# A four-layer graph network on one core: 8-bit rank rows, turns by the transposing form, gathers written out over eight buffers, scatters without a bound

## The chip, the cores and the metric

The kernel runs on one core of one Trainium2 chip. The metric is the device time of one execution in microseconds (us). Engines are named as in the profile: PE (TensorE), DVE (VectorE), ACT (ScalarE), POOL (GpSimd), SP (SyncE); "POOLq", "SPq", "ACTq" are their instruction queues, from which DMAs are issued and in which semaphores are waited for.

## The reference

There are 6250 nodes with 128 features each and 106250 edges, sorted by receiver `dst`; each node has a self-loop. Four layers follow each other, each closed by a residual and a layer norm:

```python
# L0: message = relu([h[src], h[dst], w] @ W1 + b1) @ W2 + b2; agg = segment_max(message, dst); dense update
# L1: message = relu([x[src'], factors[..]] @ Wm + bm); agg = segment_sum; dense update
# L2: attention over 4 heads: alpha = segment softmax of leaky_relu(e_l[src] + e_r[dst]); out = segment_sum(alpha * Wh[src], dst)
# L3: neigh = mean of x[src] by dst; h = relu(x @ W_in[0] + neigh @ W_in[1]); the same again with W_out
x = _layernorm(x + _L0_gnn_ref(x, edge_weight, src, dst, ...))
x = _layernorm(x + _L1_gnn_ref(x, L1_gnn_factors, src, dst, ...))
x = _layernorm(x + _L2_gnn_ref(x, edge_index, ...))
x = _layernorm(x + _L3_gnn_ref(x, L3_gnn_W_in, L3_gnn_W_out, src, dst))
```

All arithmetic is float32.

## The kernel before

Edges are cut into NB = 208 blocks of EB = 512, each of CT = 4 tiles of 128. A sweep walks the 208 blocks; a step is one block. There are five sweeps, each in one program block together with the node phase that follows it (`run(sweep, node_phase(k))`); all engines meet at a barrier between program blocks.

- Sweep k=1 (`edge_phase(1)`, layer L0, "the first sweep"): per block, POOL gathers four times 128 rows of 1 KB from `joint_table` (L1114) into one of SLOTS = 4 buffers `joint`. SP loads the rank and bar rows broadcast over 128 partitions (L1143, one DMA of 256 KB), the receiver rows (L1148, 256 KB) and the edge weights (L1155). DVE makes the 0/1 matrix `same` from rank row and `rank_cols` (L1299). PE adds up, in one bank, weight row (L1191), sender rows times the identity (L1194: turns them) and receiver rows times `same` (L1195); ACT stores the factor half of the buffer back to DRAM (L1238) and applies the relu (L1241); PE multiplies by W2 (L1203), DVE scans with a running max (L1318), PE turns back (L1213), ACT copies (L1255) and stores 256 KB (L1261).
- Relation sweep (`relation_phase`, layer L1): no gather. SP issues five DMAs a step: rank row (L1357, 128 KB broadcast), a 1 KB row (L1358), receiver rows (L1359), factor rows (L1360), and the store of the scan (L1366). PE: a bf16 row product (L1390), factor rows times the identity (L1380), receiver rows times `same` (L1381), and the turn back (L1400).
- Attention sweep (`attention_phase`, L2): gathers of 528-byte rows (L1507) into 16 buffers; stretches of 8 blocks for the softmax.
- Sweeps k=4 and k=5 (`edge_phase(4)`, `edge_phase(5)`, L3): gathers of 512-byte rows (L1114) into 4 buffers, four `transpose` (L1187), a scan, the turn back and the store.

`steps` runs an engine's pieces with lags in a hardware loop; `straight` writes them out. POOL's sweeps run in such loops, with the four index columns of a block copied by ACT into `idx` first (L1226, L1612) and handed over by the semaphores `e_idx` and `t_idx`. In the first sweep POOL waits, before it gathers into a buffer, for `e_gath_free` (L1108) and for the factor store out of that buffer (`factor_out`, L1112).

Node phases: POOL gathers each node's last scan row (L738), as soon as enough blocks are stored (`e_kept`); dense products and layer norm; tables to DRAM; for k = 0, 1, 2 a scatter of the receivers' rows to each segment's first place in `first_d` (L747, with a bounds check, so that the rows of the 22 padding nodes are dropped) and 7 gathers (L761). POOL's scatters and gathers of a node phase are written out.

A matmul of 128 float32 columns times the identity is two PE instructions here; a `transpose` is one (the counts of L1194 and L1187 in the profile: 1664 each, for one and for two sweeps of 832 tiles).

## Time and profile before

| | |
|---|---|
| median of 3 runs | 5793.68 us (5790.52 to 5794.18) |
| the profiled execution | 5795.6 us |
| its span, first to last instruction | 5793.8 us |
| mean granted TensorE clock | 0.735 of full |
| busy share: PE, DVE, ACT, POOL | 59%, 42%, 24%, 63% |
| DMA | 1127.80 MB, mean 195 GB/s |

The stages follow each other in time: preparation and node phase 0 up to 366 us, first sweep 366 to 1470, node phase 1 to 1640, relation sweep to 2228, node phase 2 to 2365, attention to 3432, node phase 3 to 3555, sweep 4 to 4593, node phase 4 to 4670, sweep 5 to 5708, node phase 5 to the end. Averages over the span mix stages with different limits, so the profile is read stage by stage. Of an engine's row, "idle before" is the time that it stood still ahead of such instructions, with what ended it.

### The profile page before, as it was taken

To read this page: it belongs to the slowest core of one execution; us is meant where nothing else is said; L and a number is where in the kernel's file an instruction comes from. 1 tells how busy PE (TensorE), PEld (TensorE's weight loads), DVE (VectorE), ACT (ScalarE), POOL (GpSimd) and SP (SyncE) were. 2 spreads that over 40 slices of the span, in tenths; PEclk is the share of its full clock that TensorE was granted. 3 is DMA by queue.
4 is the path that set the end of the run, shared out by engine and by line. 5 is a ranking of instruction groups with operands and counts; after the bars stand their busy time and mean duration, and the time that the engine had idled before them with its cause. 6 is when DMAs were issued, how large, how long until landed. Compare 5 with 4: busy or idle time off the path is not lost. (4 is left out here: it accounts for less than half of the span.)

```text
span 5793.8 us, 95902 instructions
## 1 busy us (share of the span) xinstructions
PE 3447.0 (59%) x19621; PEld 2711.1 (47%) x19621; DVE 2417.4 (42%) x3906; ACT 1387.4 (24%) x3059; POOL 3658.6 (63%) x3808
## 2 busy tenths in 40 slices
PE   1258988889669998466666662333333443333335
PEld 0246565556458886466656561333333333333333
DVE  3323333333546666366666664222222222222224
ACT  0012222222224443133333231111111211111111
POOL 2267777777611013777777774777777767777776
PEclk9779999999889999588888885555555565555557
DMA  9969999999479997466666653455544444444443
GB/s 231 306 183 291 298 300 301 304 298 296 124 234 332 327 331 231 138 182 181 181 181 186 177 168 87 131 131 131 131 131 131 124 114 131 131 131 131 131 131 106
DMA packets 809797, 1127.80 MB, mean 195 GB/s; under 512 B 128769, under 2 KB 490874, under 8 KB 806362
## 3 DMA queue, kind: packets, MB, share of 16 engines
q1 hardware_dynamic: 368424, 431.55, 24.3%
q0 software_dynamic: 134688, 305.12, 21.5%
q10 hardware_dynamic: 306588, 390.09, 20.2%
q8 instruction: 31, 0.51, 0.0%
q14 instruction: 66, 0.54, 0.0%
HBM read 688.68 MB, written 438.07 MB: 194 GB/s over the span
## 5 line engine op out<-in xcount | busy, mean ns | idle before, releaser
L1114 POOL DMA_INDIRECT gath<-sender_table,idx x1664 | 1570.2, 944 | 577.0 <-issue 413.5
L1318 DVE TENSOR_TENSOR_SCAN scan<-meta,scan,bank 128x512 f32<-128x512 bf16 x624 | 798.6, 1280 | 1943.2 <-DVEq L1315 1942.8
L1187 PE MATMUL bank<-ident,gath 128*128 128x128 f32 x1664 | 464.1, 434 | 1277.5 <-DMA gath<-sender_table,idx 1277.5
L1114 POOL DMA_INDIRECT gath<-joint_table,idx x832 | 810.4, 974 | 298.9 <-issue 208.2
L1507 POOL DMA_INDIRECT gath<-attention_table,idx x832 | 814.1, 978 | 263.3 <-issue 191.7
L1187 PEld LDWEIGHTS bank<-ident,gath 128*128 128x128 f32 x1664 | 297.8, 217 | 1443.5 <-DMA gath<-sender_table,idx 1443.5
L1255 ACT ACTIVATE rows<-bank 128x512 f32<-128x512 f32 x624 | 372.6, 597 | 1149.9 <-ACTq L1253 1121.5
L738 POOL DMA_INDIRECT gath<-scan_rows,end_i x196 | 188.9, 964 | 646.2 <-ACTq L1432 574.7
L1213 PE MATMUL bank<-ident,scan 128*128 128x128 f32 x2496 | 568.6, 373 | 4.5 <-PEq L1211 4.5
L1213 PEld LDWEIGHTS bank<-ident,scan 128*128 128x128 f32 x2496 | 470.6, 202 | 130.5 <-issue 130.5
L1194 PE MATMUL bank<-ident,gath 128*128 128x128 f32 x1664 | 372.5, 309 | 0.0
L1195 PE MATMUL bank<-same,recv 128*128 128x128 f32 x1664 | 353.4, 297 | 0.0
L1194 PEld LDWEIGHTS bank<-ident,gath 128*128 128x128 f32 x1664 | 277.4, 209 | 161.2 <-issue 161.2
L1380 PE MATMUL bank<-ident,gath 128*128 128x128 f32 x1664 | 343.2, 288 | 0.0
L1191 PE MATMUL bank<-small,w1w 1*128 1x512 f32 x416 | 236.5, 648 | 148.4 <-DMA gath<-joint_table,idx 96.5
L1543 PE MATMUL bank<-recv,same 128*128 128x4 f32 x1664 | 225.4, 259 | 156.7 <-PEq L1541 156.4
L1241 ACT ACTIVATE hid<-bank,b 128x512 f32<-128x512 f32 x208 | 143.0, 687 | 698.8 <-ACTq L1240 647.8
L1226 ACT ACTIVATE idx<-src_cols 128x4 int32 (+1 forms) x624 | 127.7, 205 | 754.5 <-ACTq L1265 651.6
L1543 PEld LDWEIGHTS bank<-recv,same 128*128 128x128 f32 x1664 | 217.9, 204 | 184.7 <-issue 184.5
L1771 DVE TENSOR_TENSOR_SCAN scan<-bank,scan,hid 128x512 f32<-128x512 f32 x208 | 266.5, 1281 | 54.6 <-DVEq L1770 46.3
L1299 DVE TENSOR_TENSOR same<-meta,rank_cols 128x512 f32<-128x512 bf16 x208 | 144.5, 695 | 346.6 <-DVEq L1298 324.7
L1195 PEld LDWEIGHTS bank<-same,recv 128*128 128x128 f32 x1664 | 282.5, 213 | 0.0
(239 smaller groups left out, 5569.5 us busy)
## 6 DMA issues: line engine op xcount, KB each, us to landing
recv<-receiver_rows SPq DMA_DIRECT2D x624, 256.0 KB
scan_rows<-rows ACTq DMA_DIRECT2D x624, 256.0 KB
attention_scan_rows<-rows ACTq DMA_DIRECT2D x208, 264.0 KB
receiver_rows<-gath ACTq DMA_DIRECT2D x26, 2048.0 KB, 12.1
meta<-edge_meta SPq DMA_DIRECT2D x208, 256.0 KB
factor_rows<-gath ACTq DMA_DIRECT2D x208, 256.0 KB
meta<-edge_meta SPq DMA_DIRECT2D x416, 128.0 KB
gath<-factor_rows SPq DMA_DIRECT2D x208, 256.0 KB
```

The lines of the kernel that those rows point to most:

```text
L1114: pool.indirect_dma_start(out=landed[s][:, c, 0:width], out_offset=None, in_=table[:, :], in_offset=bass.IndirectOffsetOnAxis(ap=idx[s][:, ...
L1187: ins = pe.transpose(b[:, c * P:(c + 1) * P], g[:, c, 0:F], ident[:, :])
L1191: pe.matmul(b[:, :], w1w[:, :], wrow[s][:, :], start=True, stop=False)
L1194: pe.matmul(o, g[:, c, 0:F], ident[:, :], start=k != 1, stop=False)
L1195: ins = pe.matmul(o, recv[s][:, c, :], same[s % 2][:, c, :], start=False, stop=k != 1 or c == CT - 1)
L1213: ins = pe.transpose(back_ps[s % 2][:, c * P:(c + 1) * P], scan[s % 2][:, c * P:(c + 1) * P], ident[:, :])
L1255: ins = act.activation(rows_flat[s][:, :, :], back_ps[s % 2][:, :].rearrange("p (c f) -> p c f", f=F), ACT.Copy)
L1318: chain(v.tensor_tensor_scan(scan[s % 2][:, :], go_on, src, scan[1 - s % 2][:, EB - 1:EB], ALU.add if k == 1 else ALU.mult, ALU.max if k = ...
L1380: pe.matmul(o, factor[s][:, c, :], ident[:, :], start=True, stop=False)
L1507: pool.indirect_dma_start(out=gath[s][:, c, :], out_offset=None, in_=att_d[:, :], in_offset=bass.IndirectOffsetOnAxis(ap=idx[s][:, c:c + 1 ...
L1543: ins = pe.matmul(er_ps[:, c * HEADS:(c + 1) * HEADS], same[s % 2][:, c, :], recv[s % SLOTS][:, c, 0:F:HID], start=True, stop=True)
L1771: chain(v.tensor_tensor_scan(scan[s % 2][:, :], fac_ps[s % 2][:, :], hid[s % 2][:, :], scan[1 - s % 2][:, EB - 1:EB], ALU.mult, ALU.add))
```

## The change

- The rank row is stored and broadcast as unsigned 8-bit numbers (`rank_d`, `rank`), 64 KB a step and not 128 KB, in three sweeps. In the first sweep the one DMA for rank and bar becomes two.
- In the first and the relation sweep, sender and factor rows are turned by matmuls with `is_transpose=True`; in the first sweep these come ahead of the weight row's product.
- POOL's four gathering sweeps are written out (`straight`), with the index columns read from `src_cols` directly; ACT's copies and their semaphores go. ACT's lags shrink by as much as they were ahead.
- `edge_phase` has RING = 8 gather buffers; receiver rows, marks and stored rows stay at 4. Node phase 1 therefore gathers into `spare`, a view of `over_head` (which POOL fills again in the relation sweep), and node phases 4 and 5 have 8 buffers and not 12.
- The scatters have no bounds check; padding nodes go to rows behind `EP`.
- Code of `edge_phase` for k = 2, which was never called, goes.

```diff
-        meta_d = dram("edge_meta", [4, EP], BF16)
+        meta_d = dram("edge_meta", [3, EP], BF16)
+        rank_d = dram("edge_rank", [1, EP], U8)
-        first_d = dram("receiver_rows", [EP, F])
+        first_d = dram("receiver_rows", [EP + NP, F])
-        joint = [... for s in range(SLOTS)]
+        joint = [... for s in range(RING)]
-        meta = [sb(f"meta{s}", [P, 3, EB], BF16) for s in range(SLOTS)]
+        meta = [sb(f"meta{s}", [P, EB], BF16) for s in range(SLOTS)]
+        rank = [sb(f"rank{s}", [P, EB], U8) for s in range(SLOTS)]
+        spare = [over_head[:, r * CT * F:(r + 1) * CT * F].rearrange("p (c f) -> p c f", f=F) for r in range(RT // CT)]
...
-            ring = {1: list(range(8, 16)), 3: list(range(NG))}.get(k, list(range(4, 16)))
+            ring = spare if k == 1 else [gath[j] for j in range(NG)] if k == 3 else gath[RING:2 * STRETCH] if k >= 4 else gath[SLOTS:2 * STRETCH]
...
-                                                in_=recv_o[s][:, c, :], in_offset=None,
-                                                bounds_check=last_row, oob_is_err=False).then_inc(scattered[s], 16)
+                                                in_=recv_o[s][:, c, :], in_offset=None).then_inc(scattered[s], 16)
...
 # edge_phase, POOL
-                    pool.wait_ge(e_idx, 1)
-                    pool.sem_inc(e_idx, -1)
                     pool.wait_ge(e_gath_free, 1)
...
                     for c in range(CT):
+                        t = (q * RING + s) * CT + c
                         pool.indirect_dma_start(out=landed[s][:, c, 0:width], out_offset=None, in_=table[:, :],
-                                                in_offset=bass.IndirectOffsetOnAxis(ap=idx[s][:, c:c + 1], axis=0)).then_inc(gathered[s], 16)
-                if k != 2:
-                    steps(pool, NB, SLOTS, (0, gather))
+                                                in_offset=bass.IndirectOffsetOnAxis(ap=src_cols[:, t:t + 1], axis=0)).then_inc(gathered[s], 16)
+                straight(NB, RING, (0, gather))
...
 # edge_phase, SP
-                    sp.dma_start(meta[s][:, lo:hi, :], meta_d[lo:hi, part(q, s, SLOTS, EB)].partition_broadcast(P)).then_inc(meta_in[s], 16)
+                    sp.dma_start(rank[s][:, :], rank_d[0, part(q, s, SLOTS, EB)].partition_broadcast(P)).then_inc(meta_in[s], 16)
+                    sp.dma_start(meta[s][:, :], meta_d[1, part(q, s, SLOTS, EB)].partition_broadcast(P)).then_inc(meta_in[s], 16)
...
 # edge_phase, PE
-                        pe.matmul(b[:, :], w1w[:, :], wrow[s][:, :], start=True, stop=False)
                     for c in range(CT):
-                        o = b[:, c * P:(c + 1) * P]
-                        pe.matmul(o, g[:, c, 0:F], ident[:, :], start=k != 1, stop=False)
-                        ins = pe.matmul(o, recv[s][:, c, :], same[s % 2][:, c, :], start=False, stop=k != 1 or c == CT - 1)
+                        pe.matmul(b[:, c * P:(c + 1) * P], g[:, c, 0:F], ident[:, :], start=c == 0, stop=False, is_transpose=True)
+                    pe.matmul(b[:, :], w1w[:, :], wrow[r][:, :], start=False, stop=False)
+                    for c in range(CT):
+                        ins = pe.matmul(b[:, c * P:(c + 1) * P], recv[r][:, c, :], same[s % 2][:, c, :], start=False, stop=c == CT - 1)
...
 # edge_phase, ACT
-                steps(act, NB, SLOTS, (4, first), *ahead, (7 if expands else 5, keep_rows), *[(0, load)] * (not expands))
+                steps(act, NB, RING, *[(0, hidden)] * expands, (3 if expands else 5, keep_rows), *[(0, load)] * (not expands))
...
 # relation_phase, POOL, SP and PE
-                pass
+                pool.memset(over_head[:, :], 0.0).then_inc(over_cleared, 1)
+                pool.wait_ge(over_cleared, 1)
+                pool.sem_inc(over_cleared, -1)
+                pool.affine_select(out=over_head[:, :], ...).then_inc(over_made, 1)
-                    sp.dma_start(meta[s][:, 1:2, :], meta_d[1:2, part(q, s, SLOTS, EB)].partition_broadcast(P)).then_inc(meta_in[s], 16)
-                    sp.dma_start(meta[s][0:1, 0:1, :], meta_d[0:1, part(q, s, SLOTS, EB)].unsqueeze(0)).then_inc(recv_in[s], 16)
+                    sp.dma_start(rank[s][:, :], rank_d[0, part(q, s, SLOTS, EB)].partition_broadcast(P)).then_inc(meta_in[s], 16)
+                    sp.dma_start(meta[s][0:1, :], meta_d[0:1, part(q, s, SLOTS, EB)]).then_inc(recv_in[s], 16)
-                        pe.matmul(o, factor[s][:, c, :], ident[:, :], start=True, stop=False)
+                        pe.matmul(o, factor[s][:, c, :], ident[:, :], start=True, stop=False, is_transpose=True)
...
 # attention_phase: POOL, ACT
-                steps(pool, NB, U, (0, gather))
+                straight(NB, U, (0, gather))
-                steps(act, NB, U, (11 + 7, keep_rows), (9 + 7, keep_weighted), (0, indices), (1 + 7, stretch))
+                steps(act, NB, U, (11, keep_rows), (9, keep_weighted), (1, stretch))
```

## Rows read from the trace of the kernel before

**Rows 1.** Windows by stage: busy us and instructions by engine, clock, DMA share, GB/s

```profile
core 0: us, PE busy (x) PEld busy (x) DVE busy (x) ACT busy (x) POOL busy (x), PEclk, DMA share, GB/s
366.20:1469.50 1103.30, 979.20 (x4930) 652.05 (x4930) 404.56 (x411) 304.04 (x612) 810.37 (x832) 0.92 0.93 294
1639.60:2228.00 588.40, 575.42 (x4360) 487.95 (x4359) 399.50 (x414) 265.20 (x413) 30.92 (x32) 1.00 0.96 325
2364.70:3432.10 1067.40, 695.21 (x5090) 642.00 (x5090) 679.45 (x1359) 316.66 (x864) 814.08 (x832) 0.81 0.64 179
3554.60:4593.00 1038.40, 405.87 (x1648) 323.12 (x1648) 264.61 (x207) 164.62 (x411) 785.07 (x832) 0.50 0.50 130
4669.80:5708.10 1038.30, 405.89 (x1648) 323.14 (x1648) 264.72 (x207) 164.55 (x411) 785.10 (x832) 0.50 0.49 130
```

**Rows 2.** Groups by line on POOL: busy us, mean ns, idle before, releasers

```profile
L1114 POOL DMA_INDIRECT gath<-sender_table,idx x1664 | 1570.2, 944 | 577.0 <-issue 413.5 <-POOLq L1108 91.1 <-ACT idx L1226 70.5
L1507 POOL DMA_INDIRECT gath<-attention_table,idx x832 | 814.1, 978 | 263.3 <-issue 191.7 <-POOLq L1505 58.0 <-ACT idx L1612 10.3
L1114 POOL DMA_INDIRECT gath<-joint_table,idx x832 | 810.4, 974 | 298.9 <-issue 208.2 <-POOLq L1112 45.3 <-POOLq L1108 21.6
...
L747 POOL DMA_INDIRECT receiver_rows<-same,start_i x147 | 149.2, 1015 | 147.6 <-POOLq L744 107.4 <-issue 38.7 <-POOLq L759 0.9
...
L462 POOL TENSOR_SCALAR_AFFINE_SELECT over_head<-over_head 128x4096 f32<-128x4096 f32 x1 | 4.5, 4550 | 0.0
L454 POOL MEMSET over_head<- 128x4096 f32 x1 | 3.5, 3507 | 0.0
```

**Rows 3.** Waits of POOL in the first sweep: us in total, times, longest

```profile
POOL gath L1114 <- POOLq L1112: 45.3, 69, 3.0
...
POOL gath L1114 <- ACT idx L1226: 9.5, 2, 6.0
```

**Rows 4.** Timeline of POOL where the attention sweep ends: start, us, idle before

```profile
3431.08 1.02 POOL L1507 DMA_INDIRECT gath<-attention_table,idx  x1 [0.30 <-issue]
3432.41 0.94 POOL L738 DMA_INDIRECT gath<-attention_scan_rows,end_i  x1 [0.31 <-POOLq L731]
```

**Rows 5.** Timeline of DVE, then of POOL, in the first sweep, same stretch

```profile
805.14 0.69 DVE L1299 TENSOR_TENSOR same<-meta,rank_cols 128x512 f32<-128x512 bf16 x1 [1.07 <-DVEq L1298]
...
804.03 0.95 POOL L1114 DMA_INDIRECT gath<-joint_table,idx  x1 [0.30 <-issue]
805.28 1.36 POOL L1114 DMA_INDIRECT gath<-joint_table,idx  x1 [0.30 <-issue]
```

**Rows 6.** Waits of SP's queue: us in total, times, longest

```profile
SPq L1356 <- SPq L1356: 21.7, 70, 3.3
...
SPq L1365 <- SPq L1365: 11.6, 6, 2.5
```

**Rows 7.** Timeline of SP's queue in the relation sweep

```profile
1906.29 0.33 SPq L1357 DMA_DIRECT2D meta<-edge_meta  x1
1906.82 0.25 SPq L1358 DMA_DIRECT2D meta<-edge_meta  x1
...
1908.35 0.36 SPq L1366 DMA_DIRECT2D scan_rows<-rows  x1
1909.13 0.33 SPq L1357 DMA_DIRECT2D meta<-edge_meta  x1
```

**Rows 8.** Timeline of PE in the relation sweep

```profile
1903.04 0.60 PE L1400 MATMUL bank<-ident,scan 128*128 128x128 f32 x4
1903.58 0.38 PE L1390 MATMUL bank<-meta,ones_row 1*128 1x512 bf16 x1
1903.89 0.49 PE L1380 MATMUL bank<-ident,gath 128*128 128x128 f32 x2
1904.21 0.39 PE L1381 MATMUL bank<-same,recv 128*128 128x128 f32 x2
1904.44 0.39 PE L1380 MATMUL bank<-ident,gath 128*128 128x128 f32 x2
```

**Rows 9.** Waits of PE in the first sweep

```profile
PE bank L1191 <- DMA gath<-joint_table,idx: 95.0, 94, 4.6
```

More of the change, by code:

```diff
@@ L139, in gnn_program @@
         w_in = sb("w_in", [P, 2, F]); w_out = sb("w_out", [P, 2, F])
-        idx = [sb(f"idx{s}", [P, CT], I32) for s in range(2 * STRETCH)]
         gath_all = sb("gath", [P, 2 * STRETCH, CT, F + HEADS])
@@ L260, in gnn_program @@
             prev_f = psb("prev_f", [P, TC])
-            goes, bar, rank_b, first_b = (carve("x", [TC, P], BF16) for _ in range(4))
+            goes, bar, first_b = (carve("x", [TC, P], BF16) for _ in range(3))
+            rank_b = carve("x", [TC, P], U8)
             begins = carve("x", [TC, P])
@@ L352, in _ @@
                         at = slice(c * P * P, (c * P + n) * P)
-                        for m, r in enumerate((goes, rank_b, bar, first_b)):
+                        for m, r in enumerate((goes, bar, first_b)):
                             sp.dma_start(meta_d[m, at].rearrange("(p k) -> p k", k=P), r[0:n, c, :]).then_inc(written, 16)
+                        sp.dma_start(rank_d[0, at].rearrange("(p k) -> p k", k=P), rank_b[0:n, c, :]).then_inc(written, 16)
                         with nc.allow_non_contiguous_dma("one word of each tile"):
@@ L1088, in edge_phase @@
         def edge_phase(k):
-            expands = k <= 2
+            expands = k == 1
             table, width = (joint_d[0:NR * P, :], 2 * F) if k == 1 else (send_d, F)
-            landed = {1: joint, 2: factor}.get(k, gath)
-            marks = {1: (1, 3), 2: (0, 2)}.get(k, (0, 1))
+            landed = joint if k == 1 else gath
             pre_ps, msg_ps, back_ps = bank[0:2], bank[2:4], bank[4:6]
@@ L1163, in sync @@
+                    sp.wait_ge(e_recv_free, 1)
+                    sp.sem_inc(e_recv_free, -1)
+                    sp.dma_start(recv[s][:, :, :], first_d[part(q, s, SLOTS, EB), :].rearrange("(p c) f -> p c f", c=CT)).then_inc(recv_in[s], 16)
+                    sp.dma_start(wrow[s][:, :], weight_d[:, part(q, s, SLOTS, EB)]).then_inc(recv_in[s], 16)
                 if expands:
-                    steps(sp, NB, SLOTS, (0, load), *[(5, store)] * (k == 2))
+                    steps(sp, NB, SLOTS, (0, load))
@@ L1222, in chain @@
                     act.sem_inc(a_done, -1)
-                def indices(q, s):
-                    act.activation(idx[s][:, :], src_cols[:, part(q, s, SLOTS, CT)], ACT.Copy).then_inc(e_idx, 1)
                 def hidden(q, s):
@@ L1608, in chain @@
                     act.sem_inc(a_done, -1)
-                def indices(q, s):
-                    act.activation(idx[s][:, :], src_cols[:, part(q, s, U, CT)], ACT.Copy).then_inc(t_idx, 1)
                 def stretch(q, s):
```

155 lines of the change are left out of this document (61 added, 94 removed).

## The prediction

> **What bounds the kernel now.** I read the windows by stage first [rows 1]. Two sweeps, 4 and 5, take 1038.4 and 1038.3 us for 832 gathers each, 1.248 us a gather; POOL is the only engine that never rests there (PE 406 us busy, DMA share 0.50). The groups of POOL [rows 2] say what the 1.248 is made of: 944 ns in the instruction and, without the 70.5 us ahead of four first gathers, (577.0 - 70.5)/1664 = 0.304 us between two. The same 0.30 stands ahead of a gather of a node phase, which is written out and not looped [rows 4]. So 832 x 1.248 = 1038 us is the least that a gathering sweep can take, and the stages to look at are those above it: the first sweep with 1103.3 and attention with 1067.4 us, and the relation sweep (588.4 us), which gathers nothing.
>
> First sweep, 65 us above the least. Busy: 810.4 against 785.1 us, 25 us more; I place it by the timeline [rows 5]: a gather that starts while DVE's compare of L1299 runs takes 1.36 and not 0.95 us. Idle: 298.9 less the 6.0 ahead of the first gather (the longest wait for an index copy) [rows 3] less 832 x 0.304 = 253, so 40 us too much. Of these, the wait for the factor store out of the buffer (L1112) has 45.3 - 69 x 0.304 = 24.3 us, the second wait for an index copy 3.5 - 0.3 = 3.2, and 12 are spread over other gaps. PE waits for landed gathers [rows 9]: POOL is behind, not PE.
>
> Attention has 29 us more busy time (814.1 against 785.1) and 263.3 - 10.3 - 253 = 0 us of idle time: 16 buffers are enough, and only the longer instructions are left.
>
> Relation sweep, 2.83 us a step. PE is busy 575 of 588 us and the DMA share is 0.96, so either looks like the bound. But SP's queue is a third: it issues five DMAs a step, from 1906.29 to 1909.13 in the rows shown [rows 7], and the waits in that queue in the whole sweep come to 21.7 us at L1356 and 11.6 at L1365 (six waits, so start and end) [rows 6]. All three are full to within some per cent.
>
> **The change part by part.** The sum is made against the profiled execution, 5795.6 us, which is 1.9 us above the median.
>
> Gathers written out, no index copies. The instruction and the 0.30 us between two stay, as written-out gathers show [rows 4]; nothing is won in sweeps 4 and 5 or in attention, except 0.3 us at each start, where POOL no longer waits for ACT. 4 x 0.3 = 1.2 us, taken as 1. The 3.2 us in the first sweep belong to the next term. The shorter lags of ACT only undo that its copies ran ahead; ACT is busy 304 of 1103 us, and in its order nothing new stands ahead of a step that POOL waits for.
>
> Eight buffers in the first sweep. A buffer's round (gather, PE, factor store, landing) now has 8 x 5.1 = 41 us and not 20. The waits at L1112 and the second index wait go: 24.3 + 3.2 = 27.5; of the other 12 us between nothing and all. What is late next: POOL itself at 1038 + 25 = 1063 us; DMA, which at 0.93 x 5.30 = 4.93 us of full work a step fits into 5.13; and PE, 979.2/208 = 4.71 us a step before the change, 4.26 after it (below). Since DMA stays near full, I take 28 us, with 0 and 40 as ends. Sweeps 4 and 5 have no idle time to give back, so their eight buffers bring 0. Node phases 4 and 5 gather 49 times 1.25 = 61 us into 8 and not 12 buffers: the ninth group of four comes 40 us after the first, long after the first can be used up, so no wait: 0, with 5 us (one group's issue) as the bad end.
>
> The transposing form. Two instructions become one for each of four tiles a step. In the relation sweep two L1381 and two L1380 alternate every 0.23 us [rows 8], so one instruction is 0.112 us; four `transpose` span 0.60 us with 0.27 us of the last one's length, 0.11 each, the same. It takes 4 x 0.112 = 0.45 us of PE a step away, at full clock, in both sweeps. In the first sweep it lies beside POOL: 0 by itself. In the relation sweep PE falls from 2.73 us a step (575.4/208 = 2.77 busy) to 2.3 and is no bound any more.
>
> 8-bit rank rows. In the relation sweep a step moves 128 + 1 + 3 x 256 = 897 KB; it becomes 833 KB. If DMA work goes by bytes its share of 0.96 falls by 7% to 0.89 at the same pace; if it goes by rows moved, by nothing. Either way SP's queue remains: five issues a step as before, of the same number of rows. What it can give back is its waiting, 21.7 us, which lies on receiver buffers coming free (L1356), that is on PE and DMA, which both get lighter. I take 12 us for the relation sweep, from 0 (the queue's own pace, rows 7, is all there is) to 26 (all waits and a part of the six at L1365). Should the new tensor need one more register instruction a step, I estimate a few hundredths of a us each, some 5 us in all, on the slow side. In the first sweep SP has one more DMA a step, 0.33 us by L1357; SP has room there. In attention (DMA share 0.64) the smaller rows bring 0. DVE's compare reads 8-bit numbers where it read bf16, 512 of them, and writes the same float32 output; taken at the same 0.69 us.
>
> POOL's filling of `over_head` costs 3.5 + 4.5 = 8 us [rows 2], beside a relation sweep of 588 us in which POOL is busy for 31: 0, since node gathers of that sweep come much later than its start.
>
> Scatters without a bound. A scatter takes 1015 ns in the mean, a gather beside a busy DVE 974 to 978 [rows 2]. Of the 147 scatters 38.7/0.304 = 127 follow the instruction before them without a wait [rows 2], so they lie on POOL's path. If the bound makes the difference of about 40 ns, that is 127 x 0.04 = 5 us; if not, 0. The 22 more rows a phase are nothing.
>
> Sum: 28 + 12 + 5 + 1 = 46 us. 5795.6 - 46 = 5749.6 for the profiled execution, 5748 for the median.
>
> **A rule weighed.** In attention half of PE's heavy instructions are transposes, and the granted clock is 0.81 in the mean [rows 1]; in the relation sweep it is 1.00, and in sweeps 4 and 5, with transposes alone and PE busy for 39% of the time, it is 0.50, the lower level of 1.2 GHz all the way. The Trainium skill, page "TensorE: Matmul & The Clock Gate", Part 4: PE-mode transpose, says that transpose work does not count as busy PE in the same way for the gate of the clock. It speaks against this change, and no row here separates it from a plain lack of work; it stands behind the clock rival below.
>
> Also, the two-input compares lengthen gathers by 25 and 29 us in two sweeps [rows 1, 2, 5]. The Trainium skill, page "GPSIMD Engine Reference", 8. Key points, puts such contention on VectorE instructions with two SBUF inputs. By it, an 8-bit input, still a second SBUF input, changes nothing.
>
> **The rivals.**
> 1. The clock falls (slower). With half of the multiplying work gone from turning, PE in the relation sweep could lose the 2.4 GHz level. For: clock 0.50 where PE only turns, 0.81 in attention [rows 1]. Against: attention keeps 0.81 with PE busy for 65% of the time, and in the relation sweep PE stays at 2.3 of 2.75 us. PE needs 2.3 us a step at full clock, so it decides below a mean clock of 2.3/2.83 = 0.81. At 0.75 a step takes 3.07 us, 0.24 x 208 = 50 us more; in the first sweep 4.26 x 0.92 / 0.75 = 5.2 us, 20 us less won. 5795.6 + 50 - 8 - 6 = 5832 us, 5830 for the median.
> 2. The first sweep is bound by DMA and not by the four buffers. For: DMA share 0.93, and the factor store that POOL waits for is itself a DMA. Against: the relation sweep runs at 0.96. Then 28 becomes 0, and 18 us remain: 5776.
> 3. Nothing moves: as 2, and SP's queue keeps the relation sweep at its pace, and the bound costs nothing. 5791.
> 4. The 8-bit rows free the gathers: the 25 + 29 us of longer instructions go as well, if the lengthening hangs on how much the compare reads. 5748 - 54 = 5694. Against: L1299 reads `rank_cols` as well, and that stays.
>
> **How the numbers follow.** Chances: the forecast 0.63 (its own range 5726 to 5766), rival 1 0.08, rival 2 0.14, rival 3 0.09, rival 4 0.06. Predicted is 5748. The best ends together (40 + 26 + 6 + 1 = 73) give 5721, and some of rival 4 reaches below; the range goes from 5714 up to rival 3, 5792, and leaves out rival 1 and most of rival 4. A change of this kernel under 0.2% (11.6 us, so above 5782) is about what a measurement can't tell from none. Faster: 0.63 + 0.14 + 0.06 = 0.83; same 0.09; slower 0.08.
>
> **What would show it.** In the profile after: sweeps 4 and 5 at 1038 us again, 1.248 a gather; attention at about 1066, with gathers of 978 ns in the mean; the first sweep at about 1075, with no wait at L1112's place above the plain 0.30; the relation sweep at about 576, with SP's queue without waits, the DMA share at 0.92 to 0.96 and a PE that waits; scatters at 944. The clock at 1.00 in the relation sweep and not under 0.85 in the first. I am wrong if the first sweep stays above 1095 (rival 2), if the clock in the relation sweep falls (rival 1), if the relation sweep comes well under 562 (then SP was no bound), or if written-out sweeps show gaps of their own, which the node phases' written-out gathers do not.

## The result

The changed kernel took 5746.58 us in the median of four runs (5743.62 to 5752.84), the kernel before 5792.10 beside it (5789.15 to 5794.18): a ratio of 0.9923, with a 95% interval of 0.9906 to 0.9940. It is faster by 45.5 us, or 0.8%; the prediction said 5748. A second comparison, on another chip, gave 5736.20 against 5787.33, 0.9913 (0.9895 to 0.9931), 51.1 us. The two profiled executions lie 52 us apart, 5795.6 and 5743.62.

Two kinds of chip turn up in the experiments. On one, the kernels here take 5736 to 5803 us in the median, on the other 7286 to 7564; what the traces show of it stands at the end. Times are compared within a kind only.

### The profile after, by stage

Windows of the changed kernel, the same stages as [rows 1]: first sweep, relation sweep (here cut from its first scan to its last), attention, sweep 4.

```profile
core 0: us, PE busy (x) PEld busy (x) DVE busy (x) ACT busy (x) POOL busy (x), PEclk, DMA share, GB/s
357.50:1424.10 1066.60, 916.42 (x4106) 551.58 (x4106) 401.29 (x410) 261.65 (x408) 813.32 (x832) 0.90 0.92 291
1600.70:2174.40 573.70, 474.28 (x3511) 381.30 (x3509) 390.91 (x414) 265.26 (x413) 31.76 (x32) 1.00 0.94 308
2307.00:3383.60 1076.60, 698.12 (x5106) 644.96 (x5107) 682.11 (x1360) 277.18 (x668) 823.15 (x832) 0.81 0.57 165
3503.00:4541.50 1038.50, 405.82 (x1648) 323.07 (x1648) 264.64 (x207) 122.39 (x205) 785.04 (x832) 0.50 0.49 130
```

Groups of POOL by line, as in [rows 2]:

```profile
L1108 POOL DMA_INDIRECT gath<-sender_table,src_cols x1664 | 1570.1, 944 | 576.3 <-issue 381.3 <-POOLq L1101 195.0
L1466 POOL DMA_INDIRECT gath<-attention_table,src_cols x832 | 823.2, 989 | 262.9 <-issue 190.5 <-POOLq L1463 67.2 <-ACTq L1595 4.6
L1108 POOL DMA_INDIRECT gath<-joint_table,src_cols x832 | 813.3, 978 | 258.9 <-issue 188.7 <-POOLq L1105 53.6 <-POOLq L1101 14.1
L748 POOL DMA_INDIRECT receiver_rows<-same,start_i x147 | 144.5, 983 | 143.5 <-POOLq L745 102.7 <-issue 39.6 <-POOLq L757 0.6
```

Measured from first to last instruction of each stage, the 52.0 us of span are made of these parts. The last three columns are the predicted gain (46 in all), the measured one, and what lies between.

| stage | before, us | after, us | predicted gain | gain | beyond |
|---|---|---|---|---|---|
| start to the first gather | 366.2 | 357.5 | 2 (of the scatters) | 8.7 | +7 |
| first sweep | 1103.3 | 1066.6 | 28 | 36.7 | +9 |
| gap behind it and node phase 1 | 148.7 | 151.1 | 1 | -2.4 | -3 |
| relation sweep, scan to scan, the gaps around it and node phase 2 | 736.5 | 722.3 | 12, and 2 of the scatters | 14.2 | 0 |
| start of attention and attention | 1077.4 | 1086.0 | 1 | -8.6 | -10 |
| the rest (sweeps 4 and 5 at 1038.3 each, node phases) | 2361.6 | 2358.2 | 0 | 3.4 | +3 |

The first sweep's POOL has no long waits left. Its waits there, as in [rows 3]; the 5.6 us are the one before the sweep's first gather:

```profile
POOL gath L1108 <- issue: 188.7, 619, 0.3
POOL gath L1108 <- POOLq L1105: 53.6, 176, 0.3
POOL gath L1108 <- POOLq L1101: 14.1, 29, 5.6
```

L1105 is the place of the old L1112 (`factor_out`). Its longest wait is 0.3 us, the plain distance between two gathers, and 258.9 - 5.6 = 253.3 us of idle time is 832 x 0.304 = 252.9 to within half a microsecond. The sweep stands on POOL's own pace.

### The profile page after: what moved, and what is told of

It is laid out like the page before. It is cut to its first block and busy times, and to the rows that moved or that the text cites. A ratio compares the mean times of both kernels' runs of the same rounds, so it can differ in the third digit from the quotient of the medians.

```text
span 5741.8 us, 88988 instructions
## 1 busy us (share of the span) xinstructions
PE 3292.9 (57%) x17957; PEld 2513.3 (44%) x17957; DVE 2408.0 (42%) x3908; ACT 1217.7 (21%) x2227; POOL 3673.6 (64%) x3810
## 5 line engine op out<-in xcount | busy, mean ns | idle before, releaser
L1108 POOL DMA_INDIRECT gath<-sender_table,src_cols x1664 | 1570.1, 944 | 576.3 <-issue 381.3
L1163 PE MATMUL bank<-ident,gath 128*128 128x128 f32 x1664 | 464.0, 434 | 1276.1 <-DMA gath<-sender_table,src_cols 1276.1
L1466 POOL DMA_INDIRECT gath<-attention_table,src_cols x832 | 823.2, 989 | 262.9 <-issue 190.5
L1108 POOL DMA_INDIRECT gath<-joint_table,src_cols x832 | 813.3, 978 | 258.9 <-issue 188.7
L1163 PEld LDWEIGHTS bank<-ident,gath 128*128 128x128 f32 x1664 | 297.7, 217 | 1442.1 <-DMA gath<-sender_table,src_cols 1442.1
L1261 DVE TENSOR_TENSOR same<-rank,rank_cols 128x512 f32<-128x512 uint8 x208 | 144.4, 694 | 412.7 <-DVEq L1260 391.1
L1730 DVE TENSOR_TENSOR_SCAN scan<-bank,scan,hid 128x512 f32<-128x512 f32 x208 | 266.6, 1282 | 55.2 <-DVEq L1729 49.3
L1170 PE MATMUL bank<-same,recv 128*128 128x128 f32 x1664 | 268.1, 310 | 0.0
L1434 DVE TENSOR_TENSOR_SCAN scan<-bank,scan,hid 128x512 f32<-128x512 f32 x208 | 265.5, 1277 | 3.5 <-DVEq L1433 2.9
L1178 PE MATMUL bank<-hid,w 128*128 128x512 f32 x416 | 249.8, 687 | 1.1 <-PEq L1177 1.1
L1554 PE MATMUL bank<-small,over_head 128*128 128x128 f32 x1664 | 244.9, 296 | 0.0
L1167 PE MATMUL bank<-ident,gath 128*128 128x128 f32 x832 | 139.5, 294 | 175.1 <-PEq L1158 154.7
```

The source lines that it names most:

```text
L1108: pool.indirect_dma_start(out=landed[s][:, c, 0:width], out_offset=None, in_=table[:, :], in_offset=bass.IndirectOffsetOnAxis(ap=src_cols[ ...
L1163: ins = pe.transpose(b[:, c * P:(c + 1) * P], g[:, c, 0:F], ident[:, :])
L1170: ins = pe.matmul(b[:, c * P:(c + 1) * P], recv[r][:, c, :], same[s % 2][:, c, :], start=False, stop=c == CT - 1)
L1178: pe.matmul(msg_ps[s % 2][:, :], w2[:, :], hid[s % 2][:, :], start=True, stop=True).then_inc(e_msg, 1)
L1434: chain(v.tensor_tensor_scan(scan[s % 2][:, :], go_ps[s % 2][:, :], hid[s % 2][:, :], scan[1 - s % 2][:, EB - 1:EB], ALU.mult, ALU.add))
L1466: pool.indirect_dma_start(out=gath[s][:, c, :], out_offset=None, in_=att_d[:, :], in_offset=bass.IndirectOffsetOnAxis(ap=src_cols[:, t:t + ...
```

## Experiments

Each kernel is the changed one with the edit shown; edits stand here without the lines around them, and what is left out of a line is marked `...`. Chips 4 (the kernel before at 7432.7 us), 5 (7442.0), 11 (7455.5) and 14 (7564.2) are of the slower kind, chip 6 of the quicker (5787.3 and 5803.4). Four of the kernels ran on chip 4 and four on chip 5, and those of one chip are compared with each other. Stages are measured from traces as above; the relation sweep always from its first scan to its last.

### The change once more, on another chip

The changed kernel again, with no edit.

> The changed kernel itself, run where the variants run, as their control: on a chip like the first one 1066.6 us in the first sweep, 573.6 us of relation sweep, 1076 in attention, 1038 in sweeps 4 and 5, ratio to the kernel before 0.992. If it falls on a chip like those of the variants so far (the kernel before at about 7435 us): ratio 0.98, first sweep 1410, relation sweep 606, attention 1585, sweeps 4 and 5 about 1238 each, as in the variants that leave these stages alone.

5736.20 us, ratio 0.9913. First sweep 1066.6 us again, relation 573.2, attention 1073.1, sweeps 4 and 5 at 1038.3 and 1038.2; 355.4 us to the first gather. Everything but the last figure repeats the first trace within 0.4 us, save attention: its gathers took 819.8 us and not 823.2.

### Four buffers

```diff
-RING = 8
+RING = 4
```

> The changed kernel with 4 gather buffers in the edge sweeps and not 8 (node phases 4 and 5 get 12 back); all else as changed. Theory (the buffers carry the gain of the first sweep): the first sweep goes back by 25 to 30 us, from 1066.6 to about 1092 to 1097, with waits of POOL for the factor store again; relation sweep unchanged at 601.6 us from the last gather of node phase 1 to the first of node phase 2's last group; time about 5773. Rival (DMA and PE relief carries it): the first sweep stays under 1075 and the time under 5756.

> The changed kernel with 4 gather buffers in the edge sweeps and not 8, once more (the first time it fell on a chip on which every kernel is a quarter slower). Theory (the buffers carry the gain of the first sweep): its first sweep is 25 us or more longer than that of the kernels of this call that have 8 buffers, with waits for the factor store. Rival (lighter DMA and PE carry it): less than 8 us longer.

Chip 4: 7308.6 us, 0.984 (0.979 to 0.989). Its first sweep took 1429.9 us; three kernels with eight buffers on that chip took 1403.4, 1406.8 and 1412.2. Chip 5: 7316.0 us, 0.983 (0.979 to 0.987), first sweep 1440.1 against 1407.4 and 1415.5 with eight buffers and the same compares. So four buffers cost 18 to 33 us on these two chips, where the theory had 25 or more. Sweep 4 took 1249.3 and 1250.3 us with four, and 1235 to 1241 with eight on the same two chips. But there the first sweep is not bound by POOL even with eight (POOL is busy for 797 to 804 us of 1400), so this size does not carry over.

What does carry over is how long a buffer is held, and that can be read on the quicker chips. In the kernel before, the median time from a block's first gather to the issue of the factor store out of the same buffer was 13.6 us. One block, from the timelines of POOL and ACT's queue in the kernel before:

```profile
1032.84 0.94 POOL L1114 DMA_INDIRECT gath<-joint_table,idx  x1 [0.68 <-POOLq L1112]
...
1046.71 0.55 ACTq L1238 DMA_DIRECT2D factor_rows<-gath  x1
...
1053.92 0.95 POOL L1114 DMA_INDIRECT gath<-joint_table,idx  x1 [1.39 <-POOLq L1112]
```

13.87 us to the issue, 7.21 more until POOL may gather into the buffer. In the 52 blocks whose first gather came late, these last took 7.1 us in the median. 13.6 + 7.1 = 20.7 us, against the 4 x 5.13 = 20.5 us that four buffers give at POOL's pace. Four buffers miss it by a little in the middle case, and in 52 of 204 blocks POOL was seen to come late. With eight the limit is 41 us, and the time to the issue could grow (16.9 us in the mean after the change, 14.9 on the other chip) without anyone waiting.

Not all of the 40 us too much was such a wait. 32.3 stood ahead of the first gather of a block, 24.2 of them with the factor store as what ended last. 7.7 stood ahead of the second gather of seven blocks, 104 gathers apart, 0.65 to 2.04 us each, where the code waits for no buffer:

```profile
663.16 0.95 POOL L1114 DMA_INDIRECT gath<-joint_table,idx  x1 [2.04 <-issue]
```

On the slower chips both kernels with four buffers and those with eight have such gaps (11 to 13 us in all), on the quicker ones the kernels with eight have none. What they wait for is not shown.

### bf16 rank rows

```diff
-        rank_d = dram("edge_rank", [1, EP], U8)
+        rank_d = dram("edge_rank", [1, EP], BF16)
-        rank = [sb(f"rank{s}", [P, EB], U8) for s in range(SLOTS)]
+        rank = [sb(f"rank{s}", [P, EB], BF16) for s in range(SLOTS)]
-            rank_b = carve("x", [TC, P], U8)
+            rank_b = carve("x", [TC, P], BF16)
```

> The changed kernel with the rank rows as bf16 again, 128 KB a step and not 64. Theory (SP's queue sets the relation sweep, POOL the first): relation within 5 us of the changed kernel's, although DMA share goes back up to 0.96; first sweep within 8 us; attention within 9 us of 1076 either way. Rival 1 (DMA sets the relation sweep): relation 10 us or more longer. Rival 2 (the 8-bit compare is what lengthened attention by 9 us): attention back at 1067.

7286.4 us, 0.9805 (0.9755 to 0.9854), the lowest ratio of the four kernels on chip 4. The relation sweep took 596.2 us against 605.5 and 607.0 in the two others that turn in the same way: with the larger rows it is 9 to 11 us quicker, which neither the theory nor a rival had. The same came out on a quicker chip, below, with what else differs.

### Plain matmuls for the turns

```diff
-  pe.matmul(b[:, c * P:(c + 1) * P], g[:, c, 0:F], ident[:, :], start=c == 0, stop=False, is_transpose=True)
+  pe.matmul(b[:, c * P:(c + 1) * P], g[:, c, 0:F], ident[:, :], start=c == 0, stop=False)
-  pe.matmul(o, factor[s][:, c, :], ident[:, :], start=True, stop=False, is_transpose=True)
+  pe.matmul(o, factor[s][:, c, :], ident[:, :], start=True, stop=False)
```

> The changed kernel with plain matmuls times the identity in place of the transposing form in the first and the relation sweep. Theory (SP's queue sets the relation sweep): relation at most 7 us longer, first sweep within 8 us. Rival (PE, at 2.73 us a step, was the bound of the relation sweep): relation back by 10 us or more. The granted clock in the first sweep rises towards the 0.92 of before.

7336.0 us, 0.9874 (0.9824 to 0.9924). The relation sweep took 623.9 us, 17 to 18 more than the 605.5 and 607.0 of its neighbours; the first sweep 1403.4, no more than theirs. The relation windows of this kernel, and of the next one, which turns by transposing, on the same chip:

```profile
2017.80:2641.70 623.90, 576.06 (x4342) 487.62 (x4340) 399.89 (x413) 265.22 (x413) 30.19 (x32) 0.97 0.88 283
```

```profile
2007.30:2614.30 607.00, 482.10 (x3514) 387.68 (x3513) 391.62 (x414) 265.45 (x413) 30.93 (x32) 0.97 0.90 291
```

PE's 94 us of work less (0.45 us in each of 208 steps, as worked out in the prediction) became 17 us of time. The theory had at most 7, so the rival came, that PE's load is a bound with the plain turns: SP waits there for 37.3 us at its loads, and for 7.3 in the next kernel (its L1320 is the same wait):

```profile
SPq L1318 <- SPq L1318: 37.3, 66, 8.6
...
SPq L1320 <- SPq L1320: 7.3, 9, 1.6
```

This is the part of the change that carries the relation sweep.

### Scatters with a bound that drops nothing

```diff
+                last_row = pool.to_reg(EP + NP - 1)
-    in_=recv_o[s][:, c, :], in_offset=None).then_inc(scattered[s], 16)
+    in_=recv_o[s][:, c, :], in_offset=None,
+    bounds_check=last_row, oob_is_err=False).then_inc(scattered[s], 16)
```

> The changed kernel with a bounds check on the scatters again (all rows lie inside the bound, so that it drops none). If the check costs what the prediction took, the scatters go from about 990 ns back to 1015 in the mean and the time by 3 to 5 us; if the earlier start of the first sweep (8.7 us) comes from it, node phase 0 shows it. Rival: no effect on the scatters' time.

7302.1 us, 0.9826 (0.9777 to 0.9875). The 147 scatters took 146.5 us, in the three neighbours without a bound 143.6, 144.1 and 144.5:

```profile
L749 POOL DMA_INDIRECT receiver_rows<-same,start_i x147 | 146.5, 996 | 197.6 <-POOLq L746 150.5 <-issue 46.7 <-POOLq L737 0.3
```

In the means that is 13 to 19 ns a scatter (996 against 977, 980 and 983). From before to after a scatter fell by 32 ns [rows 2], so the bound is about half of it; what the other half is stays open (before, the bound also dropped rows, here it drops none).

### One-input compares

```diff
-    v.tensor_tensor(same[s % 2][:, :, :], rank[s][:, :]..., rank_cols[...]..., ALU.is_equal).then_inc(e_same, 1)
+    for c in range(CT):
+        ...
+        ins = v.tensor_scalar(same[s % 2][:, c, :], rank[s][:, c * P:(c + 1) * P], rank_cols[:, col], None, ALU.is_equal)
+    ins.then_inc(e_same, 1)
```

The same in attention.

> The changed kernel with DVE's compare in the first and the attention sweep as four tensor_scalar operations, one a tile, that compare the rank row with a per-partition scalar, and not one tensor_tensor with two SBUF tensors. Theory (a gather that starts during a two-tensor compare waits for its end): no gather is lengthened in the first sweep any more, 27 us less (1066.6 to about 1040), and in attention only those at the weighing remain, 17 us less (1076 to about 1059); time about 5700. Rival 1 (any reading of SBUF by DVE in this form also holds POOL up): gathers stay long, time unchanged or worse. Rival 2 (DMA at a share of 0.93 sets the first sweep): the gathers are short again but idle time takes their place, and the sweep stays above 1060.

7329.3 us, 0.9843 (0.980 to 0.989), on chip 5. Groups of POOL by line, of this kernel and then of the next one, which has the compares as they were:

```profile
L1469 POOL DMA_INDIRECT gath<-attention_table,src_cols x832 | 802.2, 964 | 785.2 <-POOLq L1466 539.5 <-issue 244.5 <-ACTq L1598 1.2
L1108 POOL DMA_INDIRECT gath<-joint_table,src_cols x832 | 791.2, 951 | 652.8 <-issue 268.4 <-POOLq L1105 261.3 <-ACTq L1203 100.6
```

```profile
L1468 POOL DMA_INDIRECT gath<-attention_table,src_cols x832 | 815.2, 980 | 783.4 <-POOLq L1465 551.7 <-issue 231.1 <-ACTq L1597 0.6
L1109 POOL DMA_INDIRECT gath<-joint_table,src_cols x832 | 801.7, 964 | 611.3 <-issue 275.0 <-POOLq L1106 244.4 <-ACTq L1204 75.7
```

The gathers became shorter by 13 and 10.5 us: the compare does lengthen them. In the first sweep the longest falls from 1.46 to 1.05 us. What is left in attention lies at the weighing product (13.1 of 15.4 us). But four tensor_scalar of 0.30 us keep DVE busy for 42 us more in the first sweep (439.2 against 396.9), and the sweep took 1438.3 against 1407.4 us, where 27 us less were expected. That DVE's longer compare took back what the gathers gave is near at hand, but not shown. In attention, 1577.9 us against 1589.1, and 1584.8 and 1585.2 in the two others of this chip, a small gain.

How much a gather loses can be read in the kernel before, in its first sweep. One begun 0.07 us into the compare took 1.44 us, one at 0.31 us 1.21, at 0.48 us 1.03, and from 0.57 on 0.95; none of the 227 that began during a scan was longer. It loses what is left of the compare's first 0.57 us.

### One more DMA a step on SP's queue

```diff
+        again = [sb(f"again{s}", [1, EB], BF16) for s in range(SLOTS)]
+                    sp.dma_start(again[s][0:1, :], meta_d[0:1, part(q, s, SLOTS, EB)]).then_inc(recv_in[s], 16)
-                    pe.wait_ge(recv_in[s], 48)
+                    pe.wait_ge(recv_in[s], 64)
```

> The changed kernel with one more DMA of 1 KB a step on SP's queue in the relation sweep, into a tile that nobody reads. Theory (SP's queue sets the relation sweep, 573.6 us from first to last scan): one more issue costs its 0.25 us and about 0.15 of registers and start, 0.4 x 208 = 80 us less the few us that SP still waits, so the sweep is 60 to 85 us longer. Rival (DMA or PE sets it): under 15 us longer, since 1 KB beside 833 is nothing.

7375.8 us, 0.991 (0.988 to 0.994). 1 KB more a step made the relation sweep 681.3 us long: 75 us more than the 606.2 and 606.7 of two kernels on the same chip that leave this sweep alone, 0.36 us a step. The extra issue takes 0.25 us and starts 0.35 us behind the one before it; SP's queue timeline of this kernel:

```profile
2302.26 0.33 SPq L1320 DMA_DIRECT2D rank<-edge_rank  x1
2302.77 0.25 SPq L1321 DMA_DIRECT2D meta<-edge_meta  x1
2303.12 0.25 SPq L1322 DMA_DIRECT2D again<-edge_meta  x1
2303.56 0.36 SPq L1323 DMA_DIRECT2D recv<-receiver_rows  x1
```

The whole price of the issue appears in the step: with the lighter turns SP's queue is the bound here, and neither the bytes nor PE.

### The relation store issued by ACT

```diff
-                    sp.dma_start(scan_d[part(q, s, SLOTS, EB), :]..., rows_flat[s][:, :, :]).then_inc(stored[s], 16)
-                steps(sp, NB, SLOTS, (0, load), (7, store))
+                steps(sp, NB, SLOTS, (0, load))
-                    act.sem_inc(e_rows, 1)
+                    act.dma_start(scan_d[part(q, s, SLOTS, EB), :]..., rows_flat[s][:, :, :]).then_inc(stored[s], 16)
```

> The changed kernel with the relation sweep's store of scan rows issued by ACT and not by SP (0.36 us of issue and its registers leave SP's queue). Theory (SP's queue sets the sweep): the relation sweep gets 15 to 60 us shorter, down to where DMA is full (share 0.97 or more, about 2.5 us a step, 520 us). Rival (DMA or PE sets it): within 5 us of 573.6.

7350.1 us, 0.9875 (0.984 to 0.991). SP now waits for 185.2 us in the relation sweep, so its queue is relieved as meant, yet the sweep took 646.6 us, 40 more where 15 to 60 less were expected. ACT's timeline, in a quick stretch:

```profile
2306.09 0.34 ACTq L1391 DMA_DIRECT2D scan_rows<-rows  x1
2306.78 0.69 ACT L1375 ACTIVATE hid<-bank,bm 128x512 f32<-128x512 f32 x1 [0.99 <-ACTq L1374]
2308.01 0.60 ACT L1389 ACTIVATE rows<-bank 128x512 f32<-128x512 f32 x1 [0.55 <-ACTq L1387]
2308.91 0.34 ACTq L1391 DMA_DIRECT2D scan_rows<-rows  x1
```

A round of ACT is 2.82 us even here, above SP's 2.76 (573.6/208 in the changed kernel). ACT issues the store between two activations, and in this stretch each semaphore that it waits for is there when it comes; so this serial round takes the place of SP's. In the mean of this slower chip a step is 3.11 us.

Two more kernels carried this edit: one with the one-input compares too, on chip 11, and one with RING = 4 too, on chip 14.

> The changed kernel with both edits that should make it faster: the compare of the first and the attention sweep as four tensor_scalar operations, and the relation sweep's store issued by ACT. The stages are read one by one against the control (first sweep 1066.6, relation 573.4, attention 1075 us). Theory 1 (two-tensor compares lengthen gathers): first sweep about 1040, attention about 1058. Rival 1 (POOL is then held up by DMA, share 0.92): gaps take the place of the longer instructions, the first sweep stays above 1055. Theory 2 (SP's queue sets the relation sweep): 15 to 50 us less there. Rival 2 (PE and ACT set it; on the slow chips the store on ACT cost 40 us): no gain or a loss. With both theories the time is about 5650, a ratio of 0.976.

7365.95 us, 0.9884 (0.986 to 0.990). Relation 647.0 us, as without the compares' edit; first sweep 1451.1, attention 1562.5. The edits don't add up to a gain: the ratio of 0.976 that both theories together gave did not come.

> The changed kernel with two edits in two different stages: RING = 4, so four gather buffers in the first sweep and sweeps 4 and 5 again, and the store of the relation sweep issued by ACT and no longer by SP. Stage by stage against the changed kernel (first sweep 1066.6 us, relation sweep 573.6 us from its first scan to its last), on a chip of the quicker kind. Theory of the buffers: all of the 40 us of idle time that went from the first sweep hung on the four buffers; it is 1095 to 1108 us again, with the waits for a factor store back ahead of its gathers. Rival: writing the gathers out, or the lighter PE, did a part of it; then 1066 to 1085. Theory of SP's queue: in the relation sweep SP never waits, and its five issues a step (2.76 us) are the bound; with four issues it rests, and the sweep goes at the DMA engines' pace, 0.95 x 2.76 = 2.62 us a step, 545 to 560 us. Rival: DMA or PE is the bound already, or ACT's order gives it back: 570 us or more. Sweeps 4 and 5: 1038 us each by both. Sum by the theories: about 15 us slower than the changed kernel, so a ratio near 0.995 to the kernel before; by both rivals near 0.993. On a chip of the slower kind, as in the other runs there: first sweep near 1435, relation sweep near 647, and it tells nothing new.

7476.1 us, 0.9884 (0.985 to 0.991). This chip is the slowest of all (sweep 4 at 1290.0 us where others have 1235 to 1250). First sweep 1475.3, relation 658.4. There is no second kernel from this chip, so it settles neither the buffers nor SP's queue.

### bf16 rank rows, and plain turns in the first sweep only

The edit of "bf16 rank rows", and

```diff
-  pe.matmul(b[:, c * P:(c + 1) * P], g[:, c, 0:F], ident[:, :], start=c == 0, stop=False, is_transpose=True)
+  pe.matmul(b[:, c * P:(c + 1) * P], g[:, c, 0:F], ident[:, :], start=c == 0, stop=False)
```

The relation sweep keeps transposing, so there the row's type is the only difference in the source from the changed kernel, and in the first sweep both are undone.

> The changed kernel with bf16 rank rows in all sweeps, and with plain matmuls times the identity in the first sweep alone; the relation sweep keeps the transposing form. Read by stage against the control on the same kind of chip (on the first kind: relation 573.4, attention 1075; on the slow kind: 606.2 and 1586). Theory (SP's queue and PE share the relation sweep, bytes count for little): relation within 4 us of the control. Rival (the smaller rows carry the relation sweep's gain): back to 585. Attention: if the 8-bit compare lengthens it, back to 1067 on the first kind of chip; if it is where gathers and compares happen to meet, anything from 1065 to 1080, with the same 0.69 us a compare.

On a quicker chip, 5742.19 us against 5803.36: 0.9897 (0.9877 to 0.9916). Windows of first sweep, relation sweep and attention:

```profile
360.10:1424.70 1064.60, 960.05 (x4874) 632.04 (x4875) 400.31 (x407) 259.00 (x403) 811.13 (x832) 0.94 0.94 303
1610.30:2174.20 563.90, 474.17 (x3515) 381.47 (x3513) 390.58 (x413) 265.42 (x413) 31.37 (x32) 1.00 0.97 337
2306.70:3374.30 1067.60, 688.79 (x5094) 634.79 (x5095) 678.57 (x1360) 276.75 (x666) 814.17 (x832) 0.81 0.64 180
```

Three things follow.

First sweep: 1064.6 us, so with eight buffers neither the 8-bit rows nor the transposing form brought anything to it. What is left of the change there is the eight buffers and the written-out gathers without index copies, and these brought nothing in sweeps 4 and 5. With the 20.7 against 20.5 us above, that puts the 37 us on the buffers, but for 3.3 us of waiting for an index copy. This is argued by what is left over and by the slower chips; the run with four buffers alone on a quick chip is missing. The plain turns show behind the sweep: node phase 1's first gather waits 24.5 us and not 16.1 (before: 13.0), as PE is further behind POOL. The time from gather to store issue was 20.7 us here in the mean, with eight buffers between them; it tells nothing of four, since with the same plain turns it was 13.9 before.

Relation sweep: 563.9 us against 573.6 and 573.2 with 8-bit rows, at a DMA share of 0.97 and 337 GB/s against 0.94 and 308. The larger rows did not slow the sweep, so bytes were no bound. SP's queue in the changed kernel:

```profile
1907.48 0.33 SPq L1319 DMA_DIRECT2D rank<-edge_rank  x1
1908.00 0.25 SPq L1320 DMA_DIRECT2D meta<-edge_meta  x1
...
1910.48 0.34 SPq L1319 DMA_DIRECT2D rank<-edge_rank  x1
```

and in this one:

```profile
1907.38 0.33 SPq L1319 DMA_DIRECT2D rank<-edge_rank  x1
1907.81 0.29 SPq L1320 DMA_DIRECT2D meta<-edge_meta  x1
...
1910.02 0.33 SPq L1319 DMA_DIRECT2D rank<-edge_rank  x1
```

From rank row to meta row 0.52 us in one and 0.43 in the other. Between them the trace has a register instruction (41 ns, with its distance 0.07) that recomputes the offset, since one byte and two bytes an element give different offsets; with bf16 both rows share one. 9.7 us over 208 steps is 0.047 us a step, about half of the 0.09 us, and the next issue indeed stands 0.03 us further off. No run changes this instruction alone, so that it carries the difference is argued from SP's full queue (13.4 us of waiting in 573.6). The kernel before had one more than this one too (its rows are 0.53 us apart [rows 7]), for another row of one tensor, so this is no loss against before but a gain that the 8-bit rows passed up.

Attention: 1067.6 us and 814.2 of gathers, as before the change; with 8-bit rows 1076.4 and 1073.1, with 823.2 and 819.8.

Sweeps 4 and 5 took 1040.2 us each and not 1038.3, with 946 ns a gather and not 944. The kernels with the bound, with one-input compares and with one more DMA, which have 8-bit rows, have 946 too, so it is not the type; why is open.

## Why the prediction was right, and where it was not

**First sweep.** Predicted 28 of 0 to 40, found 36.7. The mechanism was right in the main; the term was sized too small. I had taken the 27.5 us of named waits and none of the 12 spread over other gaps, "since DMA stays near full". All 40 went: idle time fell from 292.9 between gathers to 253.3, and busy time rose by 2.9. The DMA share stayed at 0.92, of a step of 5.13 us, so full work is 4.72 us a step, where the prediction had 4.93 from before (the step now moves 64 KB less). Rival 2, the DMA bound, is dead: with bf16 rows the share was 0.94 at the same pace. The floor of 1063 us that the prediction named was met within 4. Of the 40 us, 7.7 were no waits for a buffer (above), so part of the gain was right by a cause that the prediction did not name.

**Relation sweep.** Predicted 12, at about 576 us; found 11.7 from first to last scan (585.3 to 573.6). Waits in SP's queue fell from 21.7 us at the loads [rows 6] and 6.8 at the store (three of the six of [rows 6] lie inside the sweep) to

```profile
SPq L1327 <- SPq L1327: 7.2, 4, 2.3
SPq L1318 <- SPq L1318: 6.2, 9, 1.6
```

and in the 400 us from 1700 to 2100 from 8.6 to 1.3 us. PE waits, 203 times for 97.5 us:

```profile
PE bank L1352 <- PEq L1351: 97.5, 203, 2.1
```

PE's busy time is 474.3/208 = 2.28 us a step, as worked out. The step's claim that both lighter loads would free the receivers' buffers held only for PE: the plain turns cost 17 us on a slower chip, while with bf16 rows the sweep was quicker. The register instruction, which I had put down as a possible 5 us on the slow side, goes with 9.7 us, and was there before.

**Scatters.** Predicted 5: 147 of them fell from 149.2 to 144.5 us, 4.7 (4.0 on the other chip). The size is right, the reason only in part, since the bound by itself is 13 to 19 of the 32 ns. The sign named for it, scatters at 944 ns, did not come: they take 983 and 987.

**Attention.** Predicted 0, lost 9.0 (5.7 on the other chip). This is the step that failed. All of it is in the length of the gathers. The prediction took this length as fixed at [rows 2]'s 978 ns because the compare still takes 0.69 us, which it does. But a gather is lengthened by how it falls beside the compare or the weighing product, and that hangs on the phase of two rhythms: in the four traces of quick chips 184 to 194 gathers are longer than 0.97 us, with 8-bit rows by 0.19 us each, with bf16 rows by 0.14 to 0.15. At the same place in the compare the loss is the same with either type (begun 0.35 us into it, a gather takes 1.16 us with 8 bits and with bf16), so a slower 8-bit compare is not the reason. Here are DVE and POOL of the changed kernel in attention, same stretch:

```profile
2708.46 0.69 DVE L1639 TENSOR_TENSOR same<-rank,rank_cols 128x512 f32<-128x512 uint8 x1
...
2707.31 0.94 POOL L1466 DMA_INDIRECT gath<-attention_table,src_cols  x1 [0.30 <-POOLq L1463]
2708.55 1.41 POOL L1466 DMA_INDIRECT gath<-attention_table,src_cols  x1 [0.30 <-issue]
2710.27 0.94 POOL L1466 DMA_INDIRECT gath<-attention_table,src_cols  x1 [0.30 <-issue]
```

The gather of 2708.55 starts 0.09 us into the compare and loses 0.47; one that starts at 0.49 us takes 1.02 and loses 0.08. The Trainium skill, page "GPSIMD Engine Reference", 8. Key points, names this contention for DVE instructions with two SBUF inputs; the run with one-input compares agrees, its gathers being 10 to 13 us shorter. That 8-bit rows shift the phase to the worse is seen in two traces against two on quick chips, and not on the slower ones (812.0 us of gathers with bf16, 810.3 to 815.7 with 8 bits), so why it does stays open. Rival 4 had it that 8-bit rows might free the gathers; it was the other way.

**Clock.** Rival 1 did not come: 1.00 in the relation sweep, with PE busy for 331 of 400 us in its middle and 391 before. The Trainium skill, page "TensorE: Matmul & The Clock Gate", Part 4: PE-mode transpose, says that transposes don't count as busy PE in the same way; twice as many of them as before did not cost the relation sweep its clock. In the first sweep it was 0.90 with transposes and 0.94 with plain turns, but with less and more work, so the two are not told apart there, and POOL waited for PE in neither.

**Not named at all.** 6.7 us less ahead of the first scatter, in a stage whose code does nearly the same. In the traces of the changed kernel and its variants this stretch ends between 266.3 and 282.7 us, so nothing can be made of 275.2 before and 268.5 after. Behind the first sweep, 3 us came back: with eight buffers POOL ends further ahead of PE, and node phase 1 waits for the end of the chain.

```profile
1423.16 0.94 POOL L1108 DMA_INDIRECT gath<-joint_table,src_cols  x1 [0.30 <-issue]
1440.21 0.94 POOL L739 DMA_INDIRECT over_head<-scan_rows,end_i  x1 [16.11 <-ACTq L1225]
```

One sum of the prediction is off by 2: of rival 3 there is 1 us left, so its time is 5792.7 for the median and not 5791.

So 46 was near 45.5 partly by luck: 9 us too little in the first sweep stand against 10 too much in attention. And the 45.5 is of medians; the two profiled executions, which the table adds up, lie 52 apart, and the medians of the other chip 51.

A kernel with bf16 rank rows and the transposing form in both sweeps would, by these rows, have the relation sweep at 564, attention at 1067, the first sweep at 1065 and the short gap behind it. With sweeps 4 and 5 at 1040.2 that is an estimated 13 to 17 us better than the changed kernel. On chip 4 it had the lowest ratio of its four, though the intervals overlap; on a quick one it has not been run.

## What to carry to other kernels

Count how long a buffer is held, to its last reader's landing, and compare it with buffers times the pace of the engine that fills them: here 20.7 stood against 20.5 us, in a sweep that lost 40 us in 1103. Count the instructions of an issuing queue, registers included, as if it were an engine: five DMAs and their offsets became the bound of a sweep that looked bound by PE and DMA, once PE had less to do, and rows of half the size made it no faster, while with a shared offset it was. An engine whose instructions are lengthened by another's is a term that moves when anything moves, so give it a range.

## What the runs showed of the hardware

A chip can be 28% slower in the same kernel. The kernel before took 7433 us on chip 4, 5792 on a quick one. There the engines' own instructions are as long as ever (a gather of sweeps 4 and 5 has 943 to 946 ns, POOL's distance between two is mostly 0.30), but register, branch and semaphore instructions come in bursts of 0.7 us each. Of more than 0.3 us there are 1027 to 1197 of ACT's in a trace, 733 to 857 us in all, nearly all in sweeps 4 and 5, where ACT issues the DMAs; and 333 to 437 of SP's, 221 to 297 us, in the three sweeps where SP does. In the traces of quick chips SP has none, and ACT one of 0.31 us. DMA issues stretch with them.

These bursts are not all of it. PE, DVE and ACT also stand still for stretches ahead of which the profile shows no wait: longer than 0.7 us, 236 to 294 times on PE, 1150 to 1470 us in all, and up to 49 us each. On quick chips PE has none and DVE two at most. POOL, whose sweeps are written out, has 81 to 103 of them, 116 to 154 us; its other long waits are for the looping engines. Up to the first scatter the slower chips lose nothing (266.3 to 282.7 us, where quick ones have 266.6 to 275.2). ACT in sweep 4, first the changed kernel on a quick chip, then the kernel with the bound on chip 4:

```profile
3601.76 0.60 ACT L1226 ACTIVATE rows<-bank 128x512 f32<-128x512 f32 x1 [4.38 <-ACTq L1224]
3602.68 0.36 ACTq L1228 DMA_DIRECT2D scan_rows<-rows  x1
3603.28 0.34 ACTq L1235 DMA_DIRECT2D meta<-edge_meta  x1
```

```profile
4635.41 0.60 ACT L1228 ACTIVATE rows<-bank 128x512 f32<-128x512 f32 x1 [3.97 <-issue]
4640.91 0.69 ACTq L1230 DMA_DIRECT2D scan_rows<-rows  x1
4643.72 1.41 ACTq L1237 DMA_DIRECT2D meta<-edge_meta  x1
4647.30 0.60 ACT L1228 ACTIVATE rows<-bank 128x512 f32<-128x512 f32 x1 [11.29 <-issue]
```

The two issues of 0.36 and 0.34 us take 0.69 and 1.41, and sweep 4 becomes 1236 us. Why was not found. The kernels with one part undone, on chip 4 and all four quicker than the one before, gained 1.3 to 2.0% there, where the whole change gains 0.8 to 0.9% on quick chips; the looping engines set more of the pace there. Which part of the change gains more by it was not tried, and no trace of the kernel before was taken on such a chip.
